# Cross-attention with a mixture of experts on one core: the expert stage run in two passes of 512 tokens, with the routing moved beside other work

## The reference

```python
# attention: queries and half of the keys from layernorm(x), the other half from the context
ln = layer_norm(_layernorm(x), g_l, b_l);  xn = layer_norm(ctx, g_x, b_x)
q = ln @ Wq;  k, v = split(concat([xn, ln], 1) @ Wkv)          # 16 heads of 64, 512 keys
out = softmax(where(mask, q k^T / 8, -max)) v
x = x + layer_norm(out @ Wout, g_o, b_o)
# experts: 64 experts of inner width 64, 8 chosen for each token, and one shared expert
xf = _layernorm(x)
shared = silu(xf @ Ws_up) @ Ws_down
aff = xf @ centroids.T;  idx = top_k(aff + expert_biases, 8)
w = sigmoid(aff[idx]);  w = w / (sum(w) + 1e-8);  cw = scatter(w at idx)
routed = einsum('etd,te->td', einsum('etf,efd->etd', silu(einsum('td,edf->etf', xf, W_up)), W_down), cw)
x = x + shared + routed
```

## Time and profile before

| | us |
|---|---|
| median of 3 runs (408.18 to 409.93) | 409.61 |
| the profiled execution | 408.53 |
| its span, first to last instruction | 406.7 |

### The profile page before, as it was taken

How to read it: one execution, slowest core, us unless ns; L and a number is a source line. 1 busy time by engine, 2 the same in 40 slices (tenths; PEclk the granted TensorE clock), 3 DMA queues, 4 the chain that set the end, 5 groups by cost and what they waited for, 6 DMA issues and landing times.

```text
span 406.7 us, 7794 instructions
## 1 busy us (share of the span) xinstructions
PE 352.8 (87%) x2369; PEld 242.2 (60%) x2369; DVE 304.1 (75%) x712; ACT 269.5 (66%) x547; POOL 260.3 (64%) x348
## 2 busy tenths in 40 slices
PE   0269796999999999999999999732899999999996
PEld 0247363666666666666666666421666777777774
DVE  2889676878878778777778778428578777778895
ACT  3469686778777787786768877504586666666681
POOL 4224312878889698888587988903126777766692
PEclk9999879999999999999999999965589999999999
DMA  8300030898998989789898799930000000000001
GB/s 247 76 0 1 18 61 0 143 166 122 176 142 134 151 144 172 135 123 178 176 162 144 119 192 133 169 40 1 1 2 0 0 0 0 0 0 0 2 0 53
DMA packets 121123, 34.40 MB, mean 85 GB/s; under 512 B 110976, under 2 KB 120704, under 8 KB 121088
## 3 DMA queue, kind: packets, MB, share of 16 engines
q1 hardware_dynamic: 120656, 32.39, 46.7%
q10 hardware_dynamic: 432, 1.57, 1.2%
HBM read 8.26 MB, written 0.52 MB: 22 GB/s over the span
## 4 chain that ended last, share of the span: by engine, by line
PE 51%; DMA 14%; POOL 12%; DVE 11%; issue 6%; ACT 5%; SPq 0%; DVEq 0%; POOLq 0%; ACTq 0%
DMA pT<-p 12%; PE ps L711 10%; PE ps L712 9%; PE ps L713 9%; POOL p L409 7%; PE ps L767 6%; PE ps L811 5%; POOL p L407 5%; PE ps L952 4%; DVE v L1205 3%; DMA tok<-in_ctx 2%; PE ps L848 2%; PE ps L836 2%; PE ps L825 2%; ACT v L572 2%
## 5 line engine op out<-in xcount | busy, mean ns | idle before, releaser
L409 POOL TENSOR_TENSOR p<-prob,p 128x512 f16<-128x512 f32 x96 | 111.7, 1164 | 7.7
L1162 DVE CUSTOM_DVE_ANT_0 sc<-ps,mask_add 128x512 f32<-128x512 f32 x128 | 83.3, 689 | 34.3 <-PE ps L767 32.8
L540 ACT ACTIVATE prob<-sc,p_bias 128x512 f32<-128x512 f32 x128 | 91.6, 717 | 8.4 <-POOL p L409 6.7
L407 POOL CAST p<-prob 128x512 f16<-128x512 f32 x96 | 58.6, 611 | 51.9 <-ACT prob L540 29.2
L1355 DVE TENSOR_TENSOR h<-h,ps 128x1024 f32<-128x1024 f32 (+1 forms) x32 | 39.1, 1221 | 18.9 <-PE ps L952 17.6
L811 PE MATMUL ps<-pT,v 128*64 128x256 f16 x768 | 49.3, 279 | 4.1 <-DMA pT<-p 4.0
L811 PEld LDWEIGHTS ps<-pT,v 128*64 128x64 f16 x768 | 40.5, 111 | 9.7 <-issue 8.8
L548 ACT ACTIVATE p_bias<-neg_max,ln_range 128x2 f32<-128x2 f32 x64 | 18.5, 290 | 41.5 <-DVE neg_max L1162 41.4
L665 ACT ACTIVATE h<-ps 128x1024 f32 (+1 forms) x32 | 32.8, 1027 | 17.6 <-PE ps L713 17.6
L434 POOL CAST wu_hi<-wup_s 128x128 fp32r (+1 forms) x30 | 25.9, 864 | 25.2 <-PE ps L713 24.9
L672 ACT ACTIVATE h_hi<-h 128x1024 fp32r (+1 forms) x26 | 27.6, 1061 | 13.1 <-PE ps L713 12.1
(11 more groups left out here) (198 smaller groups left out, 787.1 us busy)
## 6 DMA issues: line engine op xcount, KB each, us to landing
wup_s<-in_L_ffn_W_up SPq DMA_DIRECT2D x8, 256.0 KB, 3.8
wdn_s<-in_L_ffn_W_down SPq DMA_DIRECT2D x8, 256.0 KB, 4.0
pT<-p SPq DMA_TRANSPOSE x96, 3.3
wkv_s<-in_L_xattn_Wkv ACTq DMA_DIRECT2D x2, 512.0 KB, 6.1
x_in<-in_x SPq DMA_DIRECT2D x2, 256.0 KB, 7.4
tok<-in_ctx SPq DMA_DIRECT2D x4, 128.0 KB, 8.1
wq_s<-in_L_xattn_Wq ACTq DMA_DIRECT2D x1, 512.0 KB, 8.4
wo_s<-in_L_xattn_Wout SPq DMA_DIRECT2D x1, 512.0 KB, 5.3
```

Of the source, the lines that this page charges most:

```text
L407: pool.tensor_copy(p16[:, t, 0, :], prob[:, t, :]).then_inc(s_phi, 1)
L409: pool.tensor_tensor(p16[:, t, 1, :], prob[:, t, :], p16[:, t, 0, :], ALU.subtract).then_inc(s_plo, 1)
L540: act.activation(prob[:, t, :], sc[:, t, :], ACT.Exp, bias=p_bias[:, t:t + 1], scale=-1.0, accum_out=p_sum[:, i % 2, t:t + 1]).then_inc(s_ ...
L1162: return dve.tensor_tensor_reduce(sc[:, t, :], ps[:, score_bank(i, t), :], mask_add[:, step(i)[2], :], -SCALE, -LEAST, ALU.add, ALU.min, n ...
```

## The change

The expert stage works on 512 tokens at a time: pass 1 is the first half with all 32 tiles, pass 2 the second half. The shared expert becomes the first entry of each pass, so a pass has 33 entries (`EACH`) and there are 66 in all. All tiles inside a pass are 512 columns wide; rings of 8 (`h`) and 4 (`h_hi`, `h_lo`) buffers replace the full-size `h`.

The routing of the first half is put into the engines' lists of steps 19 to 31, in the second half of attention (`FIRST` = 16); that of the second half into entries 0 to 23 of pass 1. Inverse square roots are now made on DVE alone (an integer start and three Newton steps), and the gates from ACT's exponential. The expert weights are loaded after steps 2, 5, ..., 23, and POOL splits all of them once, in 16 pairs of 512-column instructions, from the end of its attention work. Addresses move: among others `kv_hi` is stored with its batches exchanged (`at_hi`), and the first half's routing goes through the queries' bank.

```diff
 # SP
-                if i == STEPS // 2 + 4:
+                if i == FIRST + 2:
                     load_late()
-                if i % B == 2:
+                if i % 3 == 2 and i // 3 < PAIRS:
...
 # POOL
             for i in range(STEPS):
                 for t in range(DMA_TILES):
                     split(i, t)
+                if i == FIRST + 4:
+                    pool.wait_ge(s_late, LATE)
+                    pool.tensor_tensor(x_res[:, :, :], x_res[:, :, :],
+                                       bo_row[:, :].unsqueeze(1).broadcast_to([P, NT, P]), ALU.add).then_inc(s_xres, 1)
+                if i == FIRST + 8:
+                    split_shared()
+                if i == FIRST + 11:
+                    xf_low(0)
...
+            def split_weights(raw, hi, lo, part, n, done):
+                cut = slice(part * 4 * P, (part + 1) * 4 * P)
+                pool.tensor_copy(hi[:, cut], raw[:, cut]).then_inc(s_pchain, 1)
                 pool.wait_ge(s_pchain, n + 1)
+                pool.tensor_tensor(lo[:, cut], raw[:, cut], hi[:, cut].bitcast(F32), ALU.subtract).then_inc(done, 1)
...
+            for part in range(FT // 4):
...
+                split_weights(up_raw, wu_hi, wu_lo, part, 2 * part, s_wu)
+                split_weights(down_raw, wd_hi, wd_lo, part, 2 * part + 1, s_wd)
+            xf_low(1)
 # ACT
+            def exp_affinity(half):
+                act.wait_ge(s_biased, half + 1)
+                act.wait_ge(s_xflo, half + 1)
+                act.activation(gate[:, :, :].rearrange("p j e -> p (j e)"), ps[:, (Q_BANK, NEXT_BANK)[half], 0:4 * E],
+                               ACT.Exp, scale=-1.0).then_inc(s_expd, 1)
...
+                if i == FIRST + 12:
+                    exp_affinity(0)
                 if i + 1 < STEPS:
                     k_high(i + 1)
...
+            for n in range(-LEAD, ENTRIES - 2):
+                if n >= -2:
+                    h_high(n + 2)
+                if n + LEAD < ENTRIES:
+                    silu(n + LEAD)
+                if n == -2:
+                    evac_out(1)
+                if n == 12:
+                    evac_xf(1)
+                if n == 13:
+                    xf_high(1)
+                if n == 17:
+                    exp_affinity(1)
+                if n == EACH + 1:
+                    evac_y(0)
+            evac_y(1)
 # PE, in the loop over the steps
+                if i == FIRST + 3:
+                    pe.wait_ge(s_qlo, i // 2 + 2)
+                    turn_out(0)
...
+                if i == FIRST + 9:
+                    pe.wait_ge(s_qlo, i // 2 + 2)
+                    turn_input(0)
+                if i == FIRST + 11:
+                    pe.wait_ge(s_qlo, i // 2 + 2)
+                    affinities(0)
+                if i == FIRST + 14:
+                    pe.wait_ge(s_qlo, STEPS // 2)
+                    turn_gates(0)
+                if i == STEPS:
+                    up(0)
+                    up(1)
+            up(2)
             project(STEPS - 1)
...
             spread(1)
+            up(3)
+            spread(2)
+            up(4)
+            turn_out(1)
+            for n in range(0, ENTRIES):
+                if n + 3 < ENTRIES:
+                    spread(n + 3)
+                if n + LEAD < ENTRIES:
+                    up(n + LEAD)
+                if n == 11:
+                    turn_input(1)
+                if n == 14:
+                    affinities(1)
+                if n == 22:
+                    turn_gates(1)
+                if n == EACH + 3:
+                    turn_y(0)
+                down(n)
+            turn_y(1)
 # DVE
+            def start_root(at):
+                r, v, t = rs[:, at:at + 4], tmp[:, 0, at:at + 4], tmp[:, 1, at:at + 4]
+                chain(dve.tensor_scalar(v, mv[:, at:at + 4, 1], EPS, None, ALU.add))
+                chained()
+                chain(dve.tensor_scalar(t.bitcast(I32), v.bitcast(I32), 1, None, ALU.logical_shift_right))
+                chained()
+                chain(dve.tensor_scalar(r.bitcast(I32), t.bitcast(I32), -1, MAGIC, ALU.mult, ALU.add))
+            def newton(at, times):
+                r, v, t = rs[:, at:at + 4], tmp[:, 0, at:at + 4], tmp[:, 1, at:at + 4]
+                for _ in range(times):
+                    chained()
+                    chain(dve.scalar_tensor_tensor(out=t, in0=r, scalar=-0.5, in1=r, op0=ALU.mult, op1=ALU.mult))
+                    chained()
+                    chain(dve.tensor_tensor(t, t, v, ALU.mult))
+                    chained()
+                    chain(dve.scalar_tensor_tensor(out=r, in0=t, scalar=1.5, in1=r, op0=ALU.add, op1=ALU.mult))
...
             for i in range(1, STEPS):
...
                 if i >= 2:
                     normalise_out(i - 2)
+                if i == FIRST + 4:
+                    dve.wait_ge(s_outN, 1)
+                    moments(turned(0), 0)
+                    start_root(0)
+                if i == FIRST + 5:
+                    newton(0, 3)
+                if i == FIRST + 6:
+                    centre(0)
+                    residual(0)
+                if i == FIRST + 7:
+                    moments(x1_of(0), 4)
+                    start_root(4)
+                if i == FIRST + 8:
+                    newton(4, 3)
+                    expert_input(0)
+                if i == FIRST + 12:
+                    find(0)
+                if i == FIRST + 13:
+                    gates(0)
+                    gate_parts(0)
+                if i == FIRST + 15:
+                    take_gates(0)
...
+            for n in range(-2, ENTRIES - 2):
+                if n + 3 < ENTRIES:
+                    weigh(n + 3)
+                h_low(n + 2)
+                if n == 0:
+                    dve.wait_ge(s_outTt, 2)
+                    moments(turned(1), 8)
+                if n == 1:
+                    start_root(8)
+                if n == 2:
+                    newton(8, 2)
+                if n == 3:
+                    newton(8, 1)
+                    centre(1)
+                if n == 5:
+                    residual(1)
+                if n == 6:
+                    moments(x1_of(1), 12)
+                if n == 7:
+                    start_root(12)
+                    newton(12, 1)
+                if n == 8:
+                    newton(12, 2)
+                if n == 9:
+                    expert_input(1)
+                if n == 16:
+                    bias_affinity(1)
+                if n == 17:
+                    find(1)
+                if n == 18:
+                    gates(1)
+                if n == 19:
+                    gate_parts(1)
+                if n == 23:
+                    take_gates(1)
...
```

More of the change, by code:

```diff
@@ new lines, in affinities, with turn_gates @@
+            def affinities(half):
+                pe.wait_ge(s_centT, 1)
+                pe.wait_ge(s_xfT, half + 1)
+                bank = (Q_BANK, NEXT_BANK)[half]
+                for j in range(4):
+                    mm = pe.matmul(ps[:, bank, j * E:(j + 1) * E], xfT[:, j * P:(j + 1) * P], centT[:, :],
+                                   start=True, stop=True)
+                mm.then_inc(s_aff, 1)
+            def turn_gates(half):
+                pe.wait_ge(s_cw, half + 1)
+                t16 = ps[:, (Q_BANK, NEXT_BANK)[half], :].bitcast(F16)
+                for j in range(4):
+                    mm = pe.transpose(t16[:, j * P:(j + 1) * P],
+                                      cw16[:, j, :, :].rearrange("p a e -> p (a e)"), one16[:, :])
+                mm.then_inc(s_cwt, 1)
@@ L1247, in residual @@
             def residual(half):
-                n = 2 * half
+                at = 8 * half
                 dve.wait_ge(s_xres, 1)
```

715 lines of the change are left out of this document (273 added, 442 removed).

## The result

The changed kernel takes 428.55 us (median of 4 runs, 426.99 to 430.59) where the kernel before, measured beside it, takes 408.89 (407.76 to 409.93): a ratio of 1.0504, 95% interval 1.0461 to 1.0546 (the two medians alone divide to 1.048). It is slower, as forecast, but by 5.0% and not by 2.3%.

A forecast was written before the change was run, and what follows sets the result against it. PE was taken to bound attention and experts, with a routing hole between. A floor of 382.2 plus 8.4 and 9 in attention, 7.4 and 9 in pass 1 gave a 416.0 span, 418.9 us by the median's scale; range 396 to 430.

The forecast's parts named there:

- The floor: Whole span without any stall: last value product at 267.9, then 1.4 + 4.4 + 102.7 + 5.8, sum 382.2 us.
- The slots: Attention, routing pieces at the end of DVE's steps: 7.2 us over their room by own work, 9 by POOL collisions.
- The four-column instructions: Attention, steps 20 to 24: sign of a right forecast, DVE's small instructions at 0.5 to 1.2 us instead of 0.16.
- ACT's wait: Attention, step 28: ACT's exponential of the affinities waits for POOL's low part; 2.3 us, bounds 0 and 5.9.
- the gain at the end: End of attention: POOL, held up elsewhere, catches up behind step 31's first mask; -2.5 us, between 0 and -4.6.
- The clock: PE's fall to the 1.2 GHz level behind stalls of 3 to 5 us: some 2 us each, in a rival only.
- the second rival: Slower still: every routing piece in attention loses 2.7 us and pass 1 loses 11.7, 428.8 in all; chance 0.10.
- The wide reciprocal: Step 29 in attention: one of nine gate instructions, 3.3 us together, with some 0.42 us for 256 columns.
- Pass 1: First expert pass: 7.4 us for DVE's routing and ACT's exponential, plus 9 for DVE's collisions with POOL's weight splits.
- The first (faster): Rival: POOL and DVE hardly meet, collisions cost under 7 us; 400.9 if they cost nothing; chance 0.39.

The follow-up runs named there:

- e_warm: Changed kernel with PE given matmuls of zeros ahead of the waiting scores in steps 22, 23, 24, 25 and 30; 425.11 us, ratio 1.0433.
- e_hold: Changed kernel with POOL holding tiles back until DVE's routing piece is through, in steps 21, 22, 23, 24 and 29; 424.84 us, ratio 1.0415.
- e_holdwarm: Changed kernel with both POOL's held tiles and PE's matmuls of zeros, in other counts (11, 13, 2, 10, 20); 420.29 us, ratio 1.0323.

## Why the prediction was right and wrong

The span lies 8.8 us above its forecast. By the terms below, 6.7 of them are the clock, which had no place in the sum (half of it shown by runs, half left over by the sum), 3.3 are pass 1, and the other terms of attention came out 1.2 lower.

**The floor: right.** Pass 2 runs PE-bound at 0.228 us a matmul, and the turn of the second half starts at 296.05, 5.25 behind the last value product; with some 0.5 for the turn itself this is the 1.4 + 4.4 that was summed.

**The slots: right in sum, in part by luck.** Forecast were 7.2 + 9 = 16.2 us by which the pieces exceed their room. The waits of PE from 185 to 296, grouped (us, times, longest):

```profile
PE ps L717 <- DVE neg_max L1095: 16.4, 7, 5.0
```

The collisions in them, each piece's length less its lone price, are 0.35 + 3.86 + 1.4 + 0.85 + 1.3 + 0.85 = 8.6 for steps 20 to 24 and 29 (for step 29 the reciprocal's excess is taken out), where 6 x 1.5 = 9 stood. Singly they are far from 1.5: the chain of nine lost 3.86, step 20 lost 0.35, and it is luck that such errors cancel. The other 16.4 - 8.6 = 7.8 hold the reciprocal's 1.3, which was not in the 7.2. The four-column instructions in steps 20 to 24, forecast at 0.5 to 1.2 us, took 0.15 to 1.31. The rule of the Trainium skill that the prediction named ("SBUF — State Buffer", "Who interferes with whom") is borne out by the rows of step 21, where DVE's three long instructions end within 0.02 us of POOL's, but a rule on who waits gives no price: POOL's gaps and its lateness do.

**ACT's wait and the gain at the end: right mechanism.** 1.6 for 2.3; and from step 31's first mask (279.2 by its read-out) to the last value product 11.6 us, before 267.9 - 253.1 = 14.8, so -3.2 for -2.5.

**The clock: the step that failed.** With these terms as measured, 16.4 + 1.6 + 1.4 - 3.2 = 16.2 of attention's 22.9; 6.7 are missing. In its sum the prediction put PE's fall to the low clock at nothing. It named a price, "some 2" for each fall (which no row of the kernel before gives), but in the second rival alone, with a chance of 0.10, though its own sum made the waits behind steps 21 and 29 2.6 and 4.1 us long. Four falls came. Length times one less granted clock, over 203 to 209, 221 to 225, 232 to 236 and 272 to 277, gives 1.5 + 1.1 + 1.6 + 1.7 + 2.3 = 8.2, a bound from above, since part of it is idle time.

That the clock is a cause, and no symptom, steps 25 and 30 show, which hold no routing piece of DVE and follow a long wait. Step 30 takes 5.1 us before, 7.1 after, and 5.2 in e_warm, where matmuls that compute nothing keep the clock at 1.00. Step 25 takes 5.9 before and 7.7 after; it takes 7.8 in e_hold and in e_warm, where the clock fell to 0.51 and 0.50 at its start, and 6.2 in e_holdwarm, where it did not fall. In time the zeros gave 2.9 us alone and 3.8 on top of e_hold, each known to 3 or 4. So some 3 to 4 of the 6.7 are shown by runs; the rest is what the sum leaves over. It is argued to lie behind steps 21 and 23, where a further piece follows and no period shows the clock alone.

**The wide reciprocal: a mis-sized term.** Priced at 0.42 by its width, it took 1.75, twice. The Trainium skill's page "VectorE: DVE Perf Modes", section "Walkthrough: the 8-slice pipeline in each mode", would have warned: it says that this operation runs an iterated divide with a repeat count of 8. The trace agrees that it is a different kind of instruction (1.75 beside 0.29 to 0.43 for others of its shape where POOL is idle); the count itself no run here shows.

**Pass 1: right in kind, 3.3 short.** Of 19.7 us, 10.0 go with POOL's subtractions (forecast 9 for all collisions), some 2.0 with the gates' reciprocal and table loads (1.1 for the loads alone), and 7.7 remain for DVE's other work (6.3). POOL went on splitting till 321.4, entry 6 of DVE's list and not entry 4; from its start at 286.98 it took 34.4 us for the forecast 32.8, so the collisions slowed it as well. How much the low clock at 310 to 320 adds to these numbers no run separates; that DVE is busy 9.93 of 10 us there speaks for little.

**The rivals.** The first (faster) needed small instructions at 0.2; they took up to 1.3. The second gave 428.8 and the kernel took 428.55, but not by its terms: its slots lose 2.7 each (measured 1.4 on average), its pass 1 loses 11.7, and the clock, which it named without a place in its sum, is the largest part of what the forecast missed. So the result lies where the prediction had put a chance of 0.10.

## What to carry to other kernels

Room in front of a step's first mask is room for one piece; a piece that exceeds it is paid in full, and PE's fall to the low clock comes on top, so where a sum forecasts waits of several us, the clock belongs into that sum and not beside it. Work moved beside another stage is to be cut to the room of its new place and kept apart from the engine that it collides with; here the same two passes are 5.0% slower or 1.7% faster than the kernel before, by the place of the routing's small instructions, by who makes them, and by a few that were left out or replaced. An edit that frees one of two coupled engines (DVE from POOL, or PE from its clock) shows less than its worth when made alone: the other limit moves in.

## What the runs showed of the hardware that was not expected

In step 21 a chain of dependent four-column instructions beside a busy POOL settles into a beat of 1.00, 0.52 and 0.16 us: POOL's next instruction starts in the hop between two of DVE's (at 199.95, where DVE's end at 200.01 and start at 200.05). Independent instructions need not fare better, four of them took 3.95 us for 1.13. POOL is slowed too: a subtraction of weights took up to 1.79 us where 1.27 is its usual time. A POOL instruction on four columns takes 0.20 us, 0.28 with its hop. Behind waits of 4.99, 1.92, 2.12 and 4.70 us PE ran at the 1.2 GHz level for a while, behind one of 1.60 it did not, and matmuls of zeros in the waits were enough to keep the clock at 1.00 from 190 to 290 (e_holdwarm).
